# First image of an attention and convolution kernel: projection weights in three pieces, halving moved into the convolution tiles, ones and selectors off VectorE, early products

## The reference, cut to what matters

```python
x = x + attention(group_norm(x))      # half the heads in 2x2 windows, half over pooled keys
x = x + conv3x3(relu(group_norm(x) * mask)) + bias
# attention, for xn = group_norm(x):
q, k, v   = split(xn @ h_qkv_w)       # window heads: softmax within 2x2 windows
lq        = xn @ l_q_w                # pooled heads: every pixel asks ...
lk, lv    = split(mean2x2(xn) @ l_kv_w)   # ... 256 pooled keys and values
out       = concat(window_attention @ h_proj_w + b, pooled_attention @ l_proj_w + b)
```

## Time and profile before

| | us |
|---|---|
| median of 3 runs | 359.06 |
| lowest and highest | 358.6, 359.2 |
| the profiled execution's own time | 356.05 |
| its span, first to last instruction | 354.0 |

### The profile page before, as it was taken

The page is one execution under the profiler, slowest core; times in us unless marked ns, Lnnn a source line. Parts: engine busy times, 40 slices in busy tenths (PEclk is TensorE's granted clock), DMA queues, the critical chain, the costliest instruction groups (busy, mean ns, idle before and its releaser), DMA issues.

```text
span 354.0 us, 4100 instructions
## 1 busy us (share of the span) xinstructions
PE 314.3 (89%) x1534; PEld 223.4 (63%) x1534; DVE 279.0 (79%) x518; ACT 147.7 (42%) x186; POOL 85.0 (24%) x47
## 2 busy tenths in 40 slices
PE   1887758999699899797999999979999999979995
PEld 1466534278576654576868745868687737858884
DVE  4979939998998687996879768887977758896662
ACT  1533648553663545352047864350255423031300
POOL 0454945400464020007700200009500200202000
PEclk9999699999789999996999999998999999999998
DMA  8759800029400000097011200394001001001002
GB/s 271 270 75 128 258 5 0 2 46 129 50 0 4 3 0 0 37 156 90 2 63 44 76 2 0 101 132 52 6 0 60 2 0 41 20 0 59 2 1 119
DMA packets 10340, 20.39 MB, mean 58 GB/s; under 512 B 1872, under 2 KB 4816, under 8 KB 10064
## 3 DMA queue, kind: packets, MB, share of 16 engines
q1 hardware_dynamic: 10320, 20.13, 27.6%
HBM read 7.93 MB, written 4.19 MB: 34 GB/s over the span
## 4 chain that ended last, share of the span: by engine, by line
PE 53%; DVE 19%; DMA 12%; ACT 7%; issue 4%; SPq 4%; DVEq 0%; ACTq 0%
PE slot L1064 25%; PE cps L1096 15%; PE slot L1140 7%; DMA qs<-probs 7%; DMA ks<-probs 5%; PE cps L1064 3%; ACT probs L532 3%; PE cps L1140 2%; SPq L262 2%; DVE xn_lo L670 2%; DVE v_lo L778 2%; SPq L266 2%; ACT p_w L575 1%; DVE xn L1040 1%; DMA xy<-x 1%
## 5 line engine op out<-in xcount | busy, mean ns | idle before, releaser
L353 POOL TENSOR_TENSOR probs<-q_w,k_w 128x1024 f32<-128x1024 f32 x16 | 38.5, 2434 | 85.0 <-DVE rw L741 72.7
L1096 PE MATMUL cps<-v_hi,cw_hi 128*128 128x512 f32 (+1 forms) x144 | 58.5, 406 | 0.2 <-DVE xy L849 0.2
L1096 PE MATMUL cps<-v_hi,cw_lo 128*128 128x512 f32 (+1 forms) x144 | 57.9, 402 | 0.0
L1096 PE MATMUL cps<-v_lo,cw_hi 128*128 128x512 f32 (+1 forms) x144 | 57.1, 397 | 0.0
L808 DVE TENSOR_REDUCE l_max<-slot 128x4 f32<-128x1024 f32 x32 | 37.8, 1220 | 6.6 <-PE slot L1064 6.6
L532 ACT ACTIVATE probs<-slot 128x1024 f32<-128x1024 f32 x32 | 31.5, 1023 | 14.6 <-PE slot L1064 14.5
L1064 PE MATMUL slot<-ks,qs 96*128 96x256 f32 x128 | 23.6, 333 | 12.2 <-DMA ks<-probs 5.3
L1096 PEld LDWEIGHTS cps<-v_hi,cw_hi 128*128 128x128 f32 x144 | 28.0, 194 | 10.0 <-issue 3.8
L1096 PEld LDWEIGHTS cps<-v_hi,cw_lo 128*128 128x128 f32 x144 | 27.7, 192 | 6.7 <-issue 1.3
L1064 PEld LDWEIGHTS slot<-ks,qs 96*128 96x128 f32 x128 | 21.7, 235 | 15.4 <-DMA ks<-probs 6.6
L1096 PEld LDWEIGHTS cps<-v_lo,cw_hi 128*128 128x128 f32 x144 | 27.8, 193 | 5.0
(11 more groups left out here) (188 smaller groups left out, 623.8 us busy)
## 6 DMA issues: line engine op xcount, KB each, us to landing
qs<-probs SPq DMA_DIRECT2D x24, 256.0 KB, 7.4
xy<-x SPq DMA_DIRECT2D x8, 512.0 KB, 8.1
out<-xy SPq DMA_DIRECT2D x8, 512.0 KB, 2.8
raw_cw<-conv_w SPq DMA_DIRECT2D x2, 1152.0 KB, 6.7
ks<-probs SPq DMA_DIRECT2D x12, 128.0 KB, 7.4
probs<-h_qkv SPq DMA_DIRECT2D x2, 192.0 KB, 4.5
probs<-l_kv SPq DMA_DIRECT2D x2, 128.0 KB, 4.2
probs<-selectors SPq DMA_DIRECT2D x1, 256.0 KB, 3.9
```

Of the source, the lines that this page charges most:

```text
L353: nc.gpsimd.tensor_tensor(qk[:, j].rearrange("p (n w) -> p n w", n=NW), q_w[:].rearrange("p (n w) -> p n w", n=NW), k_w[:, j * G:(j + 1) * ...
L1096: ins = nc.tensor.matmul(cps[:, pos % 2, y0 * WT:y1 * WT], (cw_hi, cw_hi, cw_lo)[part][:, k, pos, dy + 1, o * P:(o + 1) * P], (v_hi, v_lo, ...
```

## The change

What it does: the projection weights are loaded as `l_q`, `l_kv`, `h_qkv`, each piece with a semaphore and a cast of its own. The low part of `l_q` is made by GpSimd as soon as its cast is done, that of `l_kv` by VectorE after pooling, that of `h_qkv` by GpSimd once pooling has ended. VectorE normalises both tiles before it subtracts either. The ones are written by GpSimd at the start, the selectors are cast by ScalarE. Of the products of the first image, numbers 0 and 1 go to `mask` and no longer wait for the last projections. The convolution weights are not halved any more; the tiles of phase 0 are, in the copy to `v_hi` and in the subtraction to `v_lo`. `WARM[0]` is 4.

```diff
-SPLITS = (slice(WLQ, WLK), slice(WLK, WCOLS), slice(WQ, WLQ))
+POOLED, WINDOW = slice(WLK, WCOLS), slice(WQ, WLQ)
+PIECES = (slice(WLQ, WLK), POOLED, WINDOW)
+TILE_SCALE = (0.5, 1.0)
-WARM = (5, 6, 1, 4)
+WARM = (4, 6, 1, 4)
@@ SyncE
-            for c0, src in zip((WQ, WLQ, WLK), wqkv):
-                for k in range(KT):
-                    sp.dma_start(raw_w[:, k, c0:c0 + src.shape[2]], src[k]).then_inc(w_in, 16)
+            for cols, src, done in zip(PIECES, (wqkv[1], wqkv[2], wqkv[0]), w_in):
+                for k in range(KT):
+                    sp.dma_start(raw_w[:, k, cols], src[k]).then_inc(done, 16)
@@ helpers
+        def projection_low(engine, cols):
+            return engine.tensor_tensor(w_lo[:, :, cols], raw_w[:, :, cols], w_hi[:, :, cols].bitcast(F32),
+                                        ALU.subtract)
+        def product(b, j):
+            return mask[:, j] if b == 0 and j < 2 else qk[:, j]
@@ GpSimd: products, inner_weights, step, start
                 for j in range(NW):
+                    if b == 0 and j == 2:
+                        pool.wait_ge(proj_pe, 5)
                     nc.gpsimd.tensor_tensor(
-                        qk[:, j].rearrange("p (n w) -> p n w", n=NW),
+                        product(b, j).rearrange("p (n w) -> p n w", n=NW),
...
-                link(nc.gpsimd.tensor_scalar(both, both, 0.5, 0.0, ALU.mult, ALU.add), 8)
...
-                pool.wait_ge(proj_pe, b * 5 + 5)
+                if not first:
+                    pool.wait_ge(proj_pe, b * 5 + 5)
...
-            pool.wait_ge(w_split, 1)
-            for i, cols in enumerate(SPLITS):
-                if i == 1:
-                    pool.wait_ge(gn_c[0], N_GN)
-                nc.gpsimd.tensor_tensor(w_lo[:, :, cols], raw_w[:, :, cols], w_hi[:, :, cols].bitcast(F32),
-                                        ALU.subtract).then_inc(w_split, 1)
-            pool.wait_ge(w_split, 1 + len(SPLITS))
+            pool.wait_ge(zeroed, 1)
+            nc.gpsimd.memset(ks[SC:SM].bitcast(F32), 1.0).then_inc(ones, 1)
+            pool.wait_ge(ones, 1)
+            pool.wait_ge(w_high, 1)
+            projection_low(nc.gpsimd, PIECES[0]).then_inc(w_low, 1)
+            pool.wait_ge(w_high, len(PIECES))
             pool.wait_ge(pool_c, N_POOL)
+            projection_low(nc.gpsimd, WINDOW).then_inc(w_low, 1)
             pool.wait_ge(cw_in, KT * 16)
             outer_weights()
@@ ScalarE: projections, conv_high_of, step
-                    act.wait_ge(w_split, 1 + len(SPLITS))
+                    act.wait_ge(w_low, 2)
+                    act.wait_ge(w_pooled, 1)
...
-                nc.scalar.copy(v_hi[:, k, 2 * phase:2 * phase + 2].rearrange("p a b -> p (a b)"),
-                               mask[:, k]).then_inc(v_act, 1)
+                nc.scalar.activation(v_hi[:, k, 2 * phase:2 * phase + 2].rearrange("p a b -> p (a b)"), mask[:, k],
+                                     ACT.Copy, scale=TILE_SCALE[phase]).then_inc(v_act, 1)
...
-                    act.wait_ge(w_in, 3 * KT * 16)
-                    nc.scalar.copy(w_hi[:], raw_w).then_inc(w_split, 1)
+                    for cols, landed in zip(PIECES, w_in):
+                        act.wait_ge(landed, KT * 16)
+                        nc.scalar.copy(w_hi[:, :, cols], raw_w[:, :, cols]).then_inc(w_high, 1)
                     normalise_first()
+                    act.wait_ge(c_in, CONST_LOADS)
+                    nc.scalar.copy(sel[:].rearrange("p a b -> p (a b)"), raw_sel).then_inc(sel_act, 1)
@@ VectorE: conv_low, first_weights, start
-                nc.vector.tensor_tensor(v_lo[:, k, part].rearrange("p a b -> p (a b)"), mask[:, k],
-                                        v_hi[:, k, part].rearrange("p a b -> p (a b)").bitcast(F32),
-                                        ALU.subtract).then_inc(v_dve, 1)
+                nc.vector.scalar_tensor_tensor(v_lo[:, k, part].rearrange("p a b -> p (a b)"), mask[:, k],
+                                               TILE_SCALE[phase],
+                                               v_hi[:, k, part].rearrange("p a b -> p (a b)").bitcast(F32),
+                                               ALU.mult, ALU.subtract).then_inc(v_dve, 1)
...
-                link(nc.vector.tensor_scalar(both, both, 0.5, None, ALU.mult))
...
                 ins.then_inc(xn_ready, 1)
-                split_input(0, (k,))
+            split_input(0)
             pooling(0)
+            dve.wait_ge(w_high, 2)
+            projection_low(nc.vector, POOLED).then_inc(w_pooled, 1)
             query_lo(0)
-            key_lo(0)
             dve.wait_ge(c_in, CONST_LOADS)
-            nc.vector.tensor_copy(sel[:].rearrange("p a b -> p (a b)"), raw_sel).then_inc(w_ready, 1)
-            nc.vector.memset(ks[SC:SM].bitcast(F32), 1.0).then_inc(ones, 1)
             nc.vector.scalar_tensor_tensor(mwf[:, 2], mwf[:, 1], 1.0, mwf[:, 0], ALU.is_equal,
                                            ALU.mult).then_inc(w_ready, 1)
-            dve.wait_ge(w_ready, 2)
+            dve.wait_ge(w_ready, 1)
             nc.vector.tensor_scalar(mwf[:, 2], mwf[:, 2], -LIN, None, ALU.mult).then_inc(w_ready, 1)
-            dve.wait_ge(w_ready, 3)
+            key_lo(0)
+            dve.wait_ge(w_ready, 2)
             front(0, first=True)
@@ TensorE
-                    pe.wait_ge(w_split, 3)
+                    pe.wait_ge(w_pooled, 1)
...
-                    pe.wait_ge(w_split, 4)
+                    pe.wait_ge(w_low, 2)
...
                 if first:
+                    pe.wait_ge(sel_act, 1)
                     turned_weights()
...
-            pe.wait_ge(w_split, 2)
+            pe.wait_ge(w_high, 1)
+            pe.wait_ge(w_low, 1)
```

More of the change, by code:

```diff
@@ L179, in build @@
         x_in = [[sem(f"x_in{b}_{k}") for k in range(KT)] for b in range(B)]
-        w_in, cw_in, c_in, cst_in = sem("w_in"), sem("cw_in"), sem("c_in"), sem("cst_in")
-        w_split = sem("w_split")
+        cw_in, c_in, cst_in = sem("cw_in"), sem("c_in"), sem("cst_in")
+        w_in = [sem(f"w_in{i}") for i in range(len(PIECES))]
+        w_high, w_low, w_pooled = sem("w_high"), sem("w_low"), sem("w_low_pooled")
+        sel_act = sem("sel_act")
         out_done = sem("out_done")
@@ L315, in build @@
         taps = [raw_cw[:, k].rearrange("p r d c -> p d r c") for k in range(KT)]
-        CW_TURNED, CW_POOL, CW_DVE, CW_ACT = 10, 12, 6, 6
+        CW_TURNED, CW_POOL, CW_DVE, CW_ACT = 9, 11, 5, 6
+        def projection_low(engine, cols):
+            return engine.tensor_tensor(w_lo[:, :, cols], raw_w[:, :, cols], w_hi[:, :, cols].bitcast(F32),
+                                        ALU.subtract)
         def weight_low(engine, k, pos, tap):
             return engine.tensor_tensor(cw_lo[:, k, pos], taps[k][:, tap], cw_hi[:, k, pos].bitcast(F32), ALU.subtract)
+        def product(b, j):
+            return mask[:, j] if b == 0 and j < 2 else qk[:, j]
         def score_slot(b, i):
@@ L377, in inner_weights @@
                 pool.wait_ge(soft_c, N_SOFT)
-                t, both = taps[1], raw_cw[:, 1, :, 0:2].rearrange("p r d c -> p r (d c)")
+                t = taps[1]
                 link(nc.gpsimd.tensor_tensor(t[:, 0], t[:, 0], t[:, 2], ALU.add), 7)
-                link(nc.gpsimd.tensor_scalar(both, both, 0.5, 0.0, ALU.mult, ALU.add), 8)
                 link(nc.gpsimd.tensor_tensor(t[:, 2], t[:, 0], t[:, 1], ALU.add), 0)
@@ L777, in conv_low @@
                 part = slice(2 * phase, 2 * phase + 2)
-                nc.vector.tensor_tensor(v_lo[:, k, part].rearrange("p a b -> p (a b)"), mask[:, k],
-                                        v_hi[:, k, part].rearrange("p a b -> p (a b)").bitcast(F32),
-                                        ALU.subtract).then_inc(v_dve, 1)
+                nc.vector.scalar_tensor_tensor(v_lo[:, k, part].rearrange("p a b -> p (a b)"), mask[:, k],
+                                               TILE_SCALE[phase],
+                                               v_hi[:, k, part].rearrange("p a b -> p (a b)").bitcast(F32),
+                                               ALU.mult, ALU.subtract).then_inc(v_dve, 1)
             def first_weights():
                 link = Chain(dve, cw_dve, CW_DVE, 0)
-                t, both = taps[0], raw_cw[:, 0, :, 0:2].rearrange("p r d c -> p r (d c)")
+                t = taps[0]
                 dve.wait_ge(cw_act, 2)
@@ L1042, in _ @@
                 ins.then_inc(xn_ready, 1)
-                split_input(0, (k,))
+            split_input(0)
             pooling(0)
+            dve.wait_ge(w_high, 2)
+            projection_low(nc.vector, POOLED).then_inc(w_pooled, 1)
             query_lo(0)
-            key_lo(0)
             dve.wait_ge(c_in, CONST_LOADS)
-            nc.vector.tensor_copy(sel[:].rearrange("p a b -> p (a b)"), raw_sel).then_inc(w_ready, 1)
-            nc.vector.memset(ks[SC:SM].bitcast(F32), 1.0).then_inc(ones, 1)
             nc.vector.scalar_tensor_tensor(mwf[:, 2], mwf[:, 1], 1.0, mwf[:, 0], ALU.is_equal,
```

(7 more changed lines are left out.)

## The result

The changed kernel took 355.08 us (median of 15 runs, 352.25 to 357.81), the kernel before, run beside it, 358.34 (15 runs, 355.43 to 359.55). The ratio is 0.9932, 95% interval 0.9903 to 0.9961: a gain of under 1%, clear of the noise and larger than the forecast's 1.2. The recorded execution of the changed kernel is one of its longest, 357.61 with a span of 355.6, while that of the kernel before was one of its shortest. The two profiles laid side by side therefore say the opposite of the result, and much of what follows is about that.

A forecast was written before the change was run, and what follows sets the result against it. It took a string of dependent steps, not one full engine, as the bound. The DMA allowed 2.3, the maxima 0.8; it took 1.2, so 359.06 - 1.2 = 357.9 us, range 356.5 to 360.4.

The forecast's parts named there:

- the forecast's 1.2: Whole kernel: the gain in us, from an earlier transpose of the maxima in the first image; chance 0.4.
- the turns: First image's weights: VectorE and GpSimd instructions alternate, so maxima start at 34.4 instead of 35.20; 0.8 of 2.3 left.
- VectorE's 0.68 did go ahead of GpSimd at the end of pooling: Pooled weights' low part: VectorE's 0.69 goes first; rival with GpSimd first, 0.4 gained, 358.7, chance 0.17.
- Line 797 costs nothing: Scaled low parts of sixteen convolution tiles: same time as the old form, with 0.2 either way.
- A cost of the three casts: Start of the kernel, weights in three pieces: ScalarE's casts are covered until 10.5 and cost nothing.
- VectorE slips through: First image's weights: VectorE's fourth instruction issues before the products, maxima near 31.5; 2.3 gained, 356.8, chance 0.15.
- every shift which delays `k_w` delays the other side too: First image's weights: argument against VectorE's fourth instruction issuing before the products, which needs `k_w` some 0.4 later.
- the forecast's course: First image: VectorE's weight instructions wait twice for GpSimd's products, first maximum near 34.4, transpose near 44.1.
- The lower clock stays: Behind the first image's maxima: TensorE's clock not back by 44.1, costing 1.2 to 4, taken 2.4; 360.3, chance 0.28.
- as the same in both: Final sum: the 1.2 gain applies alike to the profiled execution (356.05) and the median (359.06).
- end at 39, no longer near the path: First image's products on GpSimd: they end at 39 instead of 42.16, off the path.

The follow-up runs named there:

- before: The kernel before the change, not edited; median 358.34 us beside the result, mean 357.74 over 98 runs.
- after: The changed kernel in its first profile, no further edit; median 355.08 us, ratio 0.9932 to the kernel before.
- after_again: The changed kernel run again with no edit; ratio 0.9951 to the kernel before.
- after_held: The changed kernel with matmuls on constants in TensorE's pauses among the score blocks, around the transpose and ahead of the values; ratio 0.9892, mean 353.19 us.
- halved_weights: The changed kernel with the halvings back in the convolution weights and tile scales of 1; ratio 0.9917, mean 355.63 us.
- after_gap: The changed kernel with two matmuls on constants filling TensorE's pause before the pooled keys' projection; ratio 0.9989, mean 356.98 us.
- gap_turn: after_gap with GpSimd's first product also waiting until VectorE's five weight instructions are done; ratio 0.9899, mean 354.29 us.
- before_again: The kernel before the change, run again with no edit; ratio 0.9997.
- late_products: The changed kernel without early products: all four wait for the fifth projection and go to their old place; ratio 0.9899, mean 354.98 us.

## Why the prediction was wrong, by its own steps

**Right: the turns and their places.** That an instruction of one engine with two inputs in SBUF waits for the running one of the other was read from two rows of before, and it gave the changed kernel's instructions to a few tenths: the pooled projection 18.50 (forecast 18.8), two weight instructions of 3.03 and 2.98, the first maximum 33.97 (34.4). One turn came the other way round: GpSimd's subtractions of the weights began first (21.74 against 21.81), so VectorE waited in its first two instructions and not in its second and third. That the third ended near 28.0 all the same (forecast 28.2) is luck. VectorE's 0.68 did go ahead of GpSimd at the end of pooling, 17.67 against 17.90. The Trainium skill's page "SBUF — State Buffer", section "Who interferes with whom", has it that the order of issue decides who is blocked. The runs agree: line 810 takes 0.96 or 3.03 by nothing but whether a product was issued first. Line 797 costs nothing, as said. A cost of the three casts would show in the start of the normalisation, and none can be told there: 10.37 to 11.33 in the profiles with them, 10.54 to 11.14 in the three without.

**Wrong: "VectorE slips through", put at 0.15.** The step that failed is the sentence against it, that every shift which delays `k_w` delays the other side too. The clock delays TensorE alone: at 0.50 through the window projections it puts `k_w` 3.1 later and VectorE's third weight instruction not at all (16.6 after the start in both). Of the four profiles with early products, the moved low parts and that pause open (after, after_again, after_held, halved_weights), three took this course. With the forecast's course forced (after_gap), the change gains 0.8 (0.3), against the 1.2 forecast; with VectorE first and TensorE's clock up (gap_turn), 3.5 (0.4), against the 2.3 of the rival. Left alone it gains 1.9, between them, as a mixture of the two courses would; how often each is taken in runs without a profile was not seen.

**Wrong: "The lower clock stays", on top of the forecast.** Its mechanism and price were right: the clock fell in the pause ahead of the fourth block, came back at 44.8, and the stretch behind took 18.43 instead of 15.53, 2.9 where 2.4 was taken. What failed is the sum. The prediction carried a gain from one execution of before to the median "as the same in both", and that execution (356.05, clock 0.963) was 1.7 under the mean of 98. Its clock stayed up behind the transpose, where that of before_again did not: there lie 2.9 of what separates the two. If before_again is the common case, as the line of span against clock suggests, the price was already in the median, and charging it to the change counted it twice. Had the recorded time of 356.05 against a median of 359.06 been read as a different course of events, not as an offset, this case would not have carried 0.28.

**The miss of 2.8 in numbers.** 0.7 is the base: 359.06 of three runs where the 15 beside the change had 358.34. 0.7 (0.4) is the gain, 1.9 instead of 1.2; after_gap, which gains 0.8 without the slip, puts it down to that. 1.4 is the draw and the measure: the two sets of 15 runs differ by 3.3 in their medians and by 2.4 in their means, all 98 and 27 runs by 1.9 in their means. So three quarters of the miss are base, luck and measure, and only a quarter is the mechanism.

**Where the change's own gain went.** From the start of the normalisation the pooled projection comes 2.4 sooner (8.13 instead of 10.53), as worked out. The products moved ahead take over half of it back at the maxima (first maximum 23.60 instead of 24.66), and late_products and gap_turn, which put VectorE first again, gain 2.8 and 3.5 on the kernel before. The forecast had priced these turns, and of the products it said that they "end at 39, no longer near the path"; their cost lay in when they start. The weights in three pieces, the copies taken off VectorE and the shorter warm-up were not taken back one by one, so what each of them is worth is not shown.

## What to carry to other kernels

Where two engines shut each other out, work that is not due soon must not start before work that is: a wait that holds GpSimd back was worth 2.7 us here, and products started 2.5 sooner ended 0.9 sooner. Before a profile is taken as the base of a sum, look how its own time stands to the runs; if it is an end of their spread, find out what happened in it that does not happen in the others, and charge that to neither kernel or to both. A change of two microseconds under a spread of six needs tens of runs, or an experiment that forces one course.

## What the runs showed of the hardware that was not expected

A lower TensorE clock brought a stage of this kernel forward: in after_again it fell behind a pause of 1.87, TensorE lost 3, and the transpose came 1.0 earlier than in after and after_gap, because two other engines met in another order. Later falls of the clock took the time back in that execution, so no single run shows a faster kernel for it; that the kernel with this pause filled is 1.1 (0.45) slower in the mean does point that way. The same pause, 1.91, left the clock at 1.00 in another execution of the same kernel, so one profile does not tell whether a pause is harmless. And a granted clock that falls need not fall in the pause: here it did between 19.5 and 20.0, when TensorE had been at work again since 18.98.
